# Whole projections behind every second attention step, and halves of them behind each

## What is computed

```
h = layernorm(xn) * ln1_g + ln1_b          # xn = normalised x, 512 x 128
q, k, v = h @ WQ + bQ, h @ WK + bK, h @ WV + bV
u = h @ Bw                                 # 512 x 64
s_t = A * s_(t-1) + u_t ;  ssm_out = states @ Cw
g = sigmoid(h @ Wg + bg)
x1 = x + g * (softmax(window(q k^T)) v @ WO + bO) + (1 - g) * ssm_out
```

## Time and profile before

| | |
|---|---|
| median of 3 runs | 1089.58 us (1087.07 to 1090.66) |
| profiled execution | 1094.57 us, of it 1092.8 us span |
| PE busy | 919.2 us, 84% of the span |
| DVE busy | 782.5 us, 72% |
| ACT busy | 712.8 us, 65% |
| POOL busy | 501.8 us, 46% |
| mean granted TensorE clock | 0.925 of full speed |

### The profile page before, as it was taken

One profiled execution on the slowest core, in us unless ns is written; L12 is line 12 of the kernel. 1 busy time (PEld: TensorE's weight loads), 2 busy tenths in 40 slices (PEclk: granted clock), 3 DMA queues, 4 the chain that ended last, 5 costly groups with the idle time before them and its releaser, 6 DMA issues.

```text
span 1092.8 us, 38402 instructions
## 1 busy us (share of the span) xinstructions
PE 919.2 (84%) x15864; PEld 561.7 (51%) x15864; DVE 782.5 (72%) x1990; ACT 712.8 (65%) x1126; POOL 501.8 (46%) x786
## 2 busy tenths in 40 slices
PE   2567898989889898988889898989888898978877
PEld 1333564646455464645555464645555464635435
DVE  4476777887877677888777777887777788656216
ACT  3205685858677595858768595867768585746645
POOL 6226355372736356273626456273635547152331
PEclk7557999999999899999999999998999999978869
DMA  5552414123332404224241503223241402310000
GB/s 108 129 118 67 93 46 105 32 94 64 100 62 75 90 27 108 50 90 62 92 75 53 112 24 109 52 90 63 75 93 36 111 17 99 58 31 6 25 1 10
DMA packets 85599, 75.24 MB, mean 69 GB/s; under 512 B 9329, under 2 KB 79154, under 8 KB 85426
## 3 DMA queue, kind: packets, MB, share of 16 engines
q1 hardware_dynamic: 83346, 72.00, 28.3%
q10 hardware_dynamic: 2080, 0.79, 0.3%
HBM read 36.33 MB, written 30.15 MB: 61 GB/s over the span
## 4 chain that ended last, share of the span: by engine, by line
PE 48%; DVE 25%; issue 13%; ACT 9%; POOL 2%; DMA 2%; DVEq 0%; SPq 0%; POOLq 0%; ACTq 0%
PE ps L558 8%; DVE mx L1074 6%; PE ps L500 6%; PE ps L690 5%; PE ps L750 5%; PE ps L711 5%; ACT pt L831 4%; PE ps L489 3%; DVE gc L1131 3%; PE ps L570 2%; DVE lin L1124 2%; PE ps L575 2%; ACT ot L836 2%; DVE junk L950 2%; PE ps L684 2%
## 5 line engine op out<-in xcount | busy, mean ns | idle before, releaser
L831 ACT ACTIVATE pt<-ps 128x1024 f32<-128x1024 f32 (+1 forms) x256 | 234.7, 917 | 212.5 <-PE ps L489 211.1
L1074 DVE TENSOR_REDUCE mx<-ps 128x2 f32<-128x320 f32 (+1 forms) x512 | 230.9, 466 | 110.6 <-PE ps L515 107.6
L1253 POOL TENSOR_SCALAR_AFFINE_SELECT pt<-pt 128x512 f32<-128x512 f32 x256 | 170.7, 669 | 264.6 <-ACT pt L831 264.3
L500 PE MATMUL ps<-kd,qz 48*32 48x160 bf16 (+1 forms) x4096 | 160.5, 241 | 66.6 <-DVE mx L1074 34.2
L489 PE MATMUL ps<-qz,kd 51*32 51x256 bf16 (+1 forms) x4096 | 183.5, 272 | 6.1 <-ACT pt L831 3.8
L558 PE MATMUL ps<-pt,va 128*32 128x256 f32 (+1 forms) x2048 | 159.8, 397 | 33.2 <-ACT ot L836 33.0
L500 PEld LDWEIGHTS ps<-kd,qz 48*32 48x32 bf16 x4096 | 72.7, 91 | 218.7 <-issue 121.3
L690 PEld LDWEIGHTS ps<-m,act_t 128*128 128x128 f32 x1024 | 126.8, 191 | 53.6 <-DVE act_t L1152 38.6
L690 PE MATMUL ps<-m,act_t 128*128 128x128 f32 x1024 | 143.2, 283 | 11.6 <-DVE act_t L1152 11.6
L1256 POOL TENSOR_SCALAR_AFFINE_SELECT pt<-pt 128x512 f32<-128x512 f32 x192 | 124.6, 649 | 0.0
L879 ACT ACTIVATE lin<-ps,mbias 128x512 f32<-128x512 f32 x128 | 87.7, 685 | 48.7 <-DVE act_t L1152 29.5
(11 more groups left out here) (158 smaller groups left out, 1672.7 us busy)
## 6 DMA issues: line engine op xcount, KB each, us to landing
qz<-qk_parts SPq DMA_DIRECT2D x32, 384.0 KB, 7.3
kd<-qk_parts SPq DMA_DIRECT2D x32, 384.0 KB, 8.7
qk_parts<-qp SPq DMA_DIRECT2D x16, 384.0 KB, 2.4
qk_parts<-kp SPq DMA_DIRECT2D x16, 384.0 KB, 2.3
xl<-L_attn_x SPq DMA_DIRECT2D x16, 256.0 KB, 3.1
qk_parts<-qp SPq DMA_DIRECT2D x16, 256.0 KB, 2.9
qk_parts<-kp SPq DMA_DIRECT2D x16, 256.0 KB, 2.7
xnr<-xn SPq DMA_DIRECT2D x16, 256.0 KB, 3.3
```

The source lines that it names most:

```text
L500: nc.tensor.matmul(ps[QG * c:QG * (c + 1), 4 + par, w * pr:w * (pr + 1)], qz[q][rows, 2 * g + pr, P * i + QG * c:P * i + QG * (c + 1)], kd ...
L831: nc.scalar.activation(to, src, ACT.Exp, scale=SCALE).then_inc(exp_ok.sem, 1)
L1074: nc.vector.tensor_reduce(mx[:, i, HG * g + pr:HG * (g + 1):2], src, AX.X, ALU.max).then_inc(mx_ok.sem, 1)
L1253: sel1 = nc.gpsimd.affine_select(out=pt[:, s, :, 0:P], in_=pt[:, s, :, 0:P], compare_op=ALU.is_ge, fill=0.0, base=0, pattern=[[0, HG], [1, ...
```

## The change

Each of `states`, q, k, u, v and g is issued in two halves of 256 rows: one half behind a step, the other behind the next. The second half, and so the signal that the projection is done, stands behind the same step as the whole did before (q 4, k 6, u 8, v 10, g 12), the first half one step earlier. `states` alone goes the other way: its first half stays behind step 0, the second goes behind step 1, and DVE's `states_in` moves from half step 2 to half step 4. `turn_h0` stays behind step 2, `turn_combine` moves from step 14 to 13. All readers but `states_in` keep their places on ACT, DVE and POOL. The wait at the head of a projection now stands at its first half.

```diff
-AT_STATES, AT_H0, AT_Q, AT_K, AT_U, AT_V, AT_G, AT_C = 0, 2, 4, 6, 8, 10, 12, 14
+HT = T // 2
+AT_STATES, AT_H0, AT_Q, AT_K, AT_U, AT_V, AT_G, AT_C = 0, 2, 3, 5, 7, 9, 11, 13
...
-                def project_k():
-                    pe.wait_ge(*done(qkr_ok, b + 2, 1))
-                    nc.tensor.matmul(bank(3), wk[:], hT[:], start=True, stop=True).then_inc(k_ps.sem, 1)
+                def project_k(half):
+                    if half == 0:
+                        pe.wait_ge(*done(qkr_ok, b + 2, 1))
+                    mm = nc.tensor.matmul(bank(3)[:, HT * half:HT * (half + 1)], wk[:], hT[:, HT * half:HT * (half + 1)], start=True, stop=True)
+                    if half:
+                        mm.then_inc(k_ps.sem, 1)
...
-                def project_v():
-                    pe.wait_ge(*done(st_ok, b + 2))
-                    for t in range(NT):
+                def project_v(half):
+                    if half == 0:
+                        pe.wait_ge(*done(st_ok, b + 2))
+                    for t in (2 * half, 2 * half + 1):
                         mm = nc.tensor.matmul(bank_t(3)[:, t], hT[:, P * t:P * (t + 1)], wv[:], start=True, stop=True)
-                    mm.then_inc(v_ps.sem, 1)
+                    if half:
+                        mm.then_inc(v_ps.sem, 1)
...
-                        if n == AT_K:
-                            project_k()
+                        if n in (AT_K, AT_K + 1):
+                            project_k(n - AT_K)
...
-                        if n == AT_K:
+                        if n == AT_K + 1:
                             qk_in(1)
...
-                        if main and step == 2 * AT_STATES + 2:
+                        if main and step == 2 * AT_STATES + 4:
                             states_in()
...
-                            if step == 2 * AT_K + 2:
+                            if step == 2 * AT_K + 4:
                                 qk_rest(1)
...
-                    if nx2 and n in (AT_Q + 2, AT_K + 2):
-                        split_rest(int(n == AT_K + 2))
+                    if nx2 and n in (AT_Q + 3, AT_K + 3):
+                        split_rest(int(n == AT_K + 3))
```

More of the change, by code:

```diff
@@ L610, in states, with project_q @@
-                def states():
-                    pe.wait_ge(*done(st_ok, b))
-                    for t in range(NT):
+                def project_q(half):
+                    if half == 0:
+                        pe.wait_ge(*done(hT_ok, b + 2))
+                    mm = nc.tensor.matmul(bank(3)[:, HT * half:HT * (half + 1)], wq[:], hT[:, HT * half:HT * (half + 1)], start=True, stop=True)
+                    if half:
+                        mm.then_inc(q_ps.sem, 1)
+                def project_k(half):
[4 more added lines that the diff above has]
+                        mm.then_inc(k_ps.sem, 1)
@@ new lines, in project_u @@
+                def project_u(half):
+                    if half == 0:
+                        pe.wait_ge(*done(qkr_ok, b + 2, 2))
+                    mm = nc.tensor.matmul(bank(3)[:, HT * half:HT * (half + 1)], bw[:], hT[:, HT * half:HT * (half + 1)], start=True, stop=True)
+                    if half:
+                        mm.then_inc(u_ps.sem, 1)
+                def project_v(half):
+                    if half == 0:
+                        pe.wait_ge(*done(st_ok, b + 2))
+                    for t in (2 * half, 2 * half + 1):
+                        mm = nc.tensor.matmul(bank_t(3)[:, t], hT[:, P * t:P * (t + 1)], wv[:], start=True, stop=True)
+                    if half:
+                        mm.then_inc(v_ps.sem, 1)
@@ new lines, in project_g, with states @@
+                def project_g(half):
+                    if half == 0:
+                        pe.wait_ge(*done(v_ok, b + 2))
+                    for t in (2 * half, 2 * half + 1):
+                        mm = nc.tensor.matmul(bank_t(3)[:, t], hT[:, P * t:P * (t + 1)], wg[:], start=True, stop=True)
+                    if half:
+                        mm.then_inc(g_ps.sem, 1)
+                def states(half):
+                    if half == 0:
+                        pe.wait_ge(*done(st_ok, b))
+                    for t in (2 * half, 2 * half + 1):
@@ L613, in states @@
                         mm = nc.tensor.matmul(bank_t(3)[:, t], st[:, b % 3, P * t:P * (t + 1)], cw[:], start=True, stop=True)
-                    mm.then_inc(cw_ps.sem, 1)
+                    if half:
+                        mm.then_inc(cw_ps.sem, 1)
                 def turn_combine():
@@ L634, in body @@
                         turn_out(b, (n - 7) // NT)
-                    if main and n == AT_STATES:
-                        states()
+                    if main and n in (AT_STATES, AT_STATES + 1):
+                        states(n - AT_STATES)
                     if nx2:
@@ L640, in body @@
                             turn_h0()
-                        if n == AT_Q:
-                            project_q()
-                        if n == AT_K:
-                            project_k()
[L645 to L650, removed]
+                        if n in (AT_Q, AT_Q + 1):
+                            project_q(n - AT_Q)
+                        if n in (AT_K, AT_K + 1):
+                            project_k(n - AT_K)
+                        if n in (AT_U, AT_U + 1):
+                            project_u(n - AT_U)
+                        if n in (AT_V, AT_V + 1):
+                            project_v(n - AT_V)
+                        if n in (AT_G, AT_G + 1):
+                            project_g(n - AT_G)
                     if nxt and n == AT_C:
@@ L841, in body @@
                             hT_in()
-                        if n == AT_Q:
+                        if n == AT_Q + 1:
                             qk_in(0)
-                        if n == AT_K:
+                        if n == AT_K + 1:
                             qk_in(1)
@@ L1082, in body @@
                                 squares(b + 2, q, (0, 1) if step == 2 * AT_SQ else (2, 3))
-                            if step == 2 * AT_Q + 2:
+                            if step == 2 * AT_Q + 4:
                                 qk_rest(0)
-                            if step == 2 * AT_K + 2:
+                            if step == 2 * AT_K + 4:
                                 qk_rest(1)
-                            if step == 2 * AT_U + 2:
+                            if step == 2 * AT_U + 4:
                                 recur()
@@ L1090, in body @@
                                 norm_f(b + 2, q, (0, 1) if step == 2 * AT_NF else (2, 3))
-                            if step == 2 * AT_V + 2:
+                            if step == 2 * AT_V + 4:
                                 v_in()
-                            if step == 2 * AT_G + 2:
+                            if step == 2 * AT_G + 4:
                                 gate_in()
```

10 lines of the change are left out of this document (removed).

## The result

The change makes the kernel slower: 1155.25 us (median of 4 runs, 1151.59 to 1162.1) against 1089.93 before, a ratio of 1.059 with a 95% interval of 1.0552 to 1.0629. The forecast was 1160 us, range 1125 to 1195. The profiled execution took 1152.91 us (span 1151.2), 58.3 more than the profiled one of before; the medians differ by 65.3.

The account below looks back on a forecast made before the run. PE was taken as nearly full in the attention stage, with work handed round between engines. Profiled 1094.6 + 53 (stages) + 1 (other passes) + 16 (clock) = 1165, less 5.0 for the median: 1160 us, range 1125 to 1195.

Parts of the forecast that it names:

- 14 x 3.8 = 53: Attention stage: 3.8 us longer in each of the 14 passes that have all parts, 53 us in sum.
- rival (A): Attention stage: halves fill PE's waits and readers are ready in time, so faster, 1064 us; decided at k; chance 0.04.
- The sign "32.5 to 33 us": Sign that the forecast is right: the attention stage takes 32.5 to 33 us at clock 1.00.
- Here is the largest term: Head of k behind step 5: PE waits 1.35 us for `qr`; step 6 starts at 12.05, before 9.31.
- 10 added stays: PE's clock: one added low-clock stay in about two passes of three, 1.6 us each, 16 us; bounds 0 to 45.
- Rival (C): Whole kernel: stages as counted, but the clock falls no more often than before, 1144 us; chance 0.21.
- 1 us for both: Passes with b below 0 and b = 14: 1 us for all of them, bounded from -2 to 5.
- The rival on the other side: The faster case, rival (A): gain only if `qk_rest(0)` ends before PE finishes step 5's scores; 1064 us, chance 0.04.

Follow-up runs that it names:

- g_late: Kernel before with g alone in halves, behind steps 12 and 13, `gate_in` at half step 27 and `turn_combine` at 14: 1079.0 us, ratio 0.9909.
- q_only: Kernel before with q alone in halves, behind steps 3 and 4: 1093.2 us, ratio 1.0048.
- k_back: Changed kernel with both halves of k behind step 6, none behind step 5: 1142.2 us, ratio 1.0478.

## Why the prediction was right

**The bound and the count.** The pitches read from the timeline carried. Step starts counted for the changed kernel and measured, from the first score: step 3 5.31 and 5.50, step 6 12.05 and 12.27, step 8 16.95 and 16.99, step 10 21.72 and 21.90, step 12 27.37 and 27.30, step 14 31.29 and 31.24, the values of step 15 34.18 and 34.06. Against the pass that I had laid out, b = 10 with 30.36, the stage is 3.7 us longer (counted 3.8); b = 10 was at the short end of the passes before, and against the usual 30.6 it is 3.5. 14 x 3.8 = 53 should have been 14 x 3.48 = 49.

That the steps agree so closely is in part luck, since two errors cancel. A half was put at 0.54 us; it takes 0.63 to 0.65 to the next scores (646.43 to 647.08 above), in g_late too. The waits were put 0.7 us too long in sum, as the next list shows. A small misreading changes nothing: the 0.37 us that rival (A) places in step 1 stand ahead of the first scores of step 2, and another 0.58 for a maximum follow there. The sign "32.5 to 33 us" is the stretch of rows 2, 29.0 us, with the 3.8 added, and not the stage up to the values of step 15.

**The waits.** Counted and measured: `turn_h0` 0.83 and 0.98, k 1.35 and 1.13, `ot` 0.89 and 0.77, v 1.08 and 1.06, `ot` 0.89 and 0.76, g 0.7 and 0.41, `turn_combine` 0.46 and 0.41. All seven are there, at the places named; their sum is 5.5 us, counted 6.2.

**The largest term.** "Here is the largest term", said of k, was wrong as a statement of worth. It is the longest wait at a head, but taking k back brings 0.65 us, no more than `states` or v, because the delay at step 6 is only in part its own. The second scores of step 6 start at 10.68 before, 11.47 in q_only, 12.13 in k_back and 12.97 in the changed kernel: q's halves add 0.79 us, the wait of `turn_h0` 0.66 and the head of k 0.84 of the 2.29. q's first half waits for nothing, as I had said, but it holds up the exponential of step 4 and with it its own read. My count has that delay in it (the exponential at 8.49), but I put the whole of it down to k.

**The clock.** I took 10 added stays at 1.6 us, 16 us. In passes 1 to 13 the clock cost some 12.6 us more than before. The low time grew from 24 to 68 us, by 44 and not by the 31 that I had put (10 x 3.1), at a smaller price: 21.9 us for 68, or 0.3 us for each microsecond and not 0.5. So here too two errors cancel. One reason for the price can be seen in the stage from 688.0 (clock 0.90): the wait of g, 0.41 us, is gone and one for `ot` is 0.5 us shorter. The stage with 0.95 from which I took 1.6 us also has a pause of PE of 0.98 us in it (ahead of 356.5) that is not the clock's. Rival (C), by which the clock would fall no more often than before, gave 1144; the low time did rise, though PE's longest wait anywhere in passes 1 to 13 is 1.3 us. So the trace disagrees with the table in the Trainium skill, "TensorE: Matmul & The Clock Gate", Part 1, by which the clock falls after an idle stretch, and agrees with the same page's section "A second HAM failure mode", by which short idle gaps between groups are enough.

**Start and end.** I put 1 us for both. They came to +5.8 (pass 0 beyond its 3.5 us of stage) and -6.3: a sum of nearly nothing out of two parts that I had not seen, which is luck. In pass 0 the clock stayed low for longer (see the last section); at the end, pass 14 has fewer low stretches than before (a stage of 27.96 against 33.13 us).

**The sum.** 53 + 1 + 16 = 70 us were forecast; the two traces differ by 58.3 us and the medians by 65.3. Both large terms were put somewhat too high, and that the time came within 5 us of the forecast owes something to the spread between executions: the traced one of before lies 4.6 us above its median, that of the changed kernel 2.3 below.

**The rival on the other side** decided where it was said to: the read of q is done at 634.33 + 0.75, 1.1 us after PE has reached the head of k. A free bank alone would not have made (A) right, as q_only shows: its first half waits for nothing and still costs. g_late wins by filling one of PE's waits with a half that neither waits nor holds up an exponential that is needed sooner.

## What to carry to other kernels

Halving a piece of in-order work to fill waits moves its first half ahead of something: count what the head of that half waits for, and then which exponential or copy now stands behind it, before counting the wait that it fills. Where all pieces pass through one buffer, the second half can only keep its place if the first finds the buffer free; moving the second half later, as in g_late, cost no such wait. And a gain at one wait is only real at the end of the chain: here a saved 0.5 us vanished into a DVE operation some steps on, until that was moved.

## What the runs showed of the hardware

The page's row of granted clock was wrong ahead of the first change that this trace records. In the changed kernel's trace it reads 9 tenths from the first slice, and the windows give 1.00 for 96 to 113, yet the values, 0.64 us at full speed, take 1.08 there:

```profile
108.18 1.08 PE L559 MATMUL ps<-pt,va 128*32 128x256 f32 x8
```

```profile
120.00 0.64 PE L559 MATMUL ps<-pt,va 128*32 128x256 f32 x8 [0.76 <-ACT ot L852]
```

Before, the same matmuls took 1.08 at 93.75 and 0.64 at 95.68. So the start ran at 1.2 GHz for at least 12 us longer, at half speed, which fits the 5.8 us that pass 0 lost beyond its waits; and the mean clocks, 0.953 after and 0.925 before, can't be compared. The same shows in the executions of the kernel before on record: their mean clock is near 0.93 in some and near 0.97 in others, at the same times (1087.9 us at 0.932, 1088.3 at 0.969).

A pair of `norm_f` took 1.51 to 1.95 us beside POOL's work on k (L1259 and L1261) and 0.97 just after it, for the same shapes, while POOL was at its masks (L1269). That the work on k slows it was not tested alone; the 0.68 us per pass that moving `norm_f` brought come from taking all of it out from ahead of `v_in`.

How often the clock falls is not set by PE's waits in a stage alone. In the changed kernel the passes from 623.5 (b = 8) and 755.3 (b = 10) have the same stage, 34.06 us, with the same waits up to the 1.3 us for `ot` in step 15. The second then falls to the low level 34.3 us after its start, and the pass takes 65.88 us; the first does not, and takes 64.51. Ten other passes have a low stretch that begins in that wait or soon behind it; three of these have one more from 23.1 us on, behind the wait for the scan, and one from 13.4 us on, behind that for q. What settles it is open.
